# Adaptive layer norm, Koopman attention and 4-bit feed-forward in one kernel: feed-forward output as features by tokens and turned back on TensorE, the inverse in a buffer of its own, a shorter basis and a shorter rounding

## The reference

```python
sa, ca, ga, sb, cb, gb = mod[:, 0], ..., mod[:, 5]
h = _layernorm(x) * (1 + ca) + sa
x = x + ga * attention(h)
h = _layernorm(x) * (1 + cb) + sb
x = x + gb * ffn(h)
```

```python
G = Kc.T @ Kc + RIDGE_EPS * I
W = jnp.linalg.solve(G, Kc.T @ Vc)
U = U0
for _ in range(POWER_K):
    U, _ = jnp.linalg.qr(W @ U)
Wr = U @ (U.T @ W)
S_new = DECAY_ALPHA * S + Wr
out = SCALE * (Qc @ S_new)
```

```python
gate = fp4_linear(x, w_gate)
y = fp4_linear(x, w_up)
h = jax.nn.silu(gate) * y
return fp4_linear(h, w_down)
```

## Time and profile before

| | us |
|---|---|
| median of three runs | 1487.51 |
| lowest, highest | 1479.54, 1488.72 |
| the profiled execution | 1489.35 |
| its span, first to last instruction | 1487.5 |
| TensorE busy | 969.3 (65%) |
| VectorE busy | 1230.2 (83%) |
| ScalarE busy | 640.3 (43%) |
| GpSimd busy | 231.3 (16%) |

### The profile page before, as it was taken

How to read it: one execution, slowest core, us unless ns; L and a number is a source line. 1 busy time by engine, 2 the same in 40 slices (tenths; PEclk the granted TensorE clock), 3 DMA queues, 4 the chain that set the end, 5 groups by cost and what they waited for, 6 DMA issues and landing times.

```text
span 1487.5 us, 43627 instructions
## 1 busy us (share of the span) xinstructions
PE 969.3 (65%) x17726; PEld 780.0 (52%) x17726; DVE 1230.2 (83%) x3729; ACT 640.3 (43%) x1294; POOL 231.3 (16%) x149
## 2 busy tenths in 40 slices
PE   1443940389177799787799787852819825996175
PEld 0332530365167667677667686742717624775154
DVE  5885659949999779996799996798875798878997
ACT  3663630156135466555466454431416512563152
POOL 3552001101111001113102023012140000021000
PEclk9855985589579899899899898785959957898597
DMA  2555110001000001001101002030030200111000
GB/s 78 168 167 194 46 44 0 1 18 50 8 4 4 4 10 46 2 4 50 54 17 38 3 4 86 4 123 0 4 125 19 75 1 17 50 47 32 9 25 24
DMA packets 52086, 61.60 MB, mean 41 GB/s; under 512 B 4048, under 2 KB 32416, under 8 KB 51888
## 3 DMA queue, kind: packets, MB, share of 16 engines
q1 hardware_dynamic: 51888, 58.84, 12.6%
HBM read 38.31 MB, written 20.51 MB: 40 GB/s over the span
## 4 chain that ended last, share of the span: by engine, by line
DVE 36%; PE 32%; issue 13%; ACT 5%; POOL 2%; DMA 1%; SPq 0%; DVEq 0%; POOLq 0%; ACTq 0%
PE a_bank L840 5%; PE a_bank L830 3%; PE a_bank L846 3%; DVE a_total L1581 3%; DVE a_outer L1579 3%; DVE a_blocks L1584 3%; DVE a_outer L1575 2%; PE a_bank L946 2%; PE a_bank L961 2%; PE a_bank L769 2%; PE a_bank L898 2%; PE a_bank L698 2%; DVE a_blocks L1586 2%; DVE a_recip L1561 2%; PE a_bank L808 2%
## 5 line engine op out<-in xcount | busy, mean ns | idle before, releaser
L1092 ACT ACTIVATE a_work<-a_bank 128x512 f32<-128x512 f32 (+1 forms) x193 | 110.9, 599 | 206.5 <-PE a_bank L808 170.8
L1485 POOL TENSOR_TENSOR a_root<-a_recip,a_half 128x32 f32<-128x32 f32 (+2 forms) x24 | 89.8, 3743 | 655.8 <-DVEq L1570 636.9
L808 PE MATMUL a_bank<-a_ident,a_blocks 128*128 128x128 f32 x256 | 42.2, 340 | 162.6 <-DVE a_blocks L1595 162.6
L1092 ACT ACTIVATE a_solve<-a_bank 128x512 f32<-128x512 f32 (+2 forms) x184 | 87.9, 522 | 114.1 <-PE a_bank L846 53.9
L1575 DVE TENSOR_TENSOR a_outer<-a_blocks,a_weight 128x62 f32<-128x62 f32 (+15 forms) x248 | 129.4, 522 | 0.0
L1581 DVE TENSOR_REDUCE a_total<-a_outer 128x62 f32<-128x62 f32 (+30 forms) x248 | 127.0, 512 | 0.3
L808 PEld LDWEIGHTS a_bank<-a_ident,a_blocks 128*128 128x128 f32 x256 | 40.4, 208 | 163.7 <-DVE a_blocks L1595 163.7
L1579 DVE TENSOR_TENSOR a_outer<-a_blocks 128x60 f32<-128x60 f32 (+14 forms) x240 | 119.2, 497 | 0.7 <-DVE a_outer L1575 0.7
L1584 DVE TENSOR_TENSOR a_blocks<-a_blocks,a_outer 128x60 f32<-128x60 f32 (+14 forms) x240 | 118.3, 493 | 0.0
L698 PE MATMUL a_bank<-a_wk,a_cg 128*128 128x512 f32 x256 | 117.3, 602 | 0.0
L769 PE MATMUL a_bank<-a_scaled,a_blocks 128*128 128x352 f32 x256 | 90.6, 495 | 28.7 <-ACT a_scaled L1072 15.2
(11 more groups left out here) (200 smaller groups left out, 2402.4 us busy)
## 6 DMA issues: line engine op xcount, KB each, us to landing
f_x<-in_L_attn_x SPq DMA_DIRECT2D x16, 256.0 KB, 3.2
s_xnt<-f_xt SPq DMA_DIRECT2D x16, 256.0 KB, 2.1
s_c<-f_cm SPq DMA_DIRECT2D x16, 256.0 KB, 2.3
s_base<-f_base SPq DMA_DIRECT2D x16, 256.0 KB, 2.8
a_cg<-s_c SPq DMA_DIRECT2D x16, 256.0 KB, 2.9
a_cc<-s_c SPq DMA_DIRECT2D x16, 256.0 KB, 3.7
a_xnt<-s_xnt SPq DMA_DIRECT2D x16, 256.0 KB, 3.9
a_base_in<-s_base SPq DMA_DIRECT2D x13, 256.0 KB, 2.6
```

Of the source, the lines that this page charges most:

```text
L808: last = nc.tensor.transpose(bank[:, i * P:(i + 1) * P], rows_[:, :, 4 * rb + i], ident[:])
L1092: nc.scalar.activation(out, view, ACT.Copy, scale=scale).then_inc(emptied, 1)
L1485: nc.gpsimd.tensor_tensor(root[:, :, a:b], recip[:, :, a:b], half[:, :, a:b], ALU.pow).then_inc(roots_ok, 1)
```

## The change

Four things change.

1. In `factor` the inverse gets a buffer of its own, `triangle`, cleared and given ones on its diagonal before the wait for the block. The weights are gone: the known rows are multiplied with `m[:, :, 0:i, i]`, numbers that earlier steps left in the matrix, one in each column. The 31 memsets are gone, and one product scales the whole result.
2. `orthogonalise` takes the square of the vector and its products with the rest in one pass, and divides the few results, not the vector.
3. `fp4_blocks` drops one instruction: the bound and the magic number go into the addition and the subtraction.
4. Feed-forward `down` makes its output as features by tokens, 512 columns at once; ScalarE scales it by `gb`, which is now a number for each partition, and TensorE adds it, turned back, onto the residual, which it has put into the bank by a product with the identity. `finish` is gone from VectorE. The step `down` is cut in two, `turn_hidden` (t) and `down` (y), and the order becomes g0, g1, t0, g2, y0, t1, g3, y1 and so on, where it was g0, g1, d0, g2, d1.

```diff
-                        row, rest = m[:, :, 0:j, j], m[:, :, 0:j, i:HB]
                         ch.wait(inverse)
...
-                        weights = ch.inc(V.scalar_tensor_tensor(weight[:, :, 0:i], m[:, :, i, 0:i], -1.0, recip[:, :, 0:i], ALU.mult, ALU.mult))
-                        column = ch.inc(V.scalar_tensor_tensor(m[:, :, j, i:HB], m[:, :, i:HB, j], -1.0, bcast(recip[:, :, j], 2, n_i), ALU.mult, ALU.mult))
-                        ch.wait(weights)
-                        terms = area(0, n_i, i)
-                        known = ch.inc(V.tensor_tensor(terms, m[:, :, i:HB, 0:i], bcast(weight[:, :, 0:i], 2, n_i), ALU.mult))
-                        if j:
-                            ch.wait(column)
-                            step = area(2 * KEPT * KEPT, j, n_i)
-                            product = ch.inc(V.tensor_tensor(step, bcast(m[:, :, j, i:HB], 2, j), bcast(row, 3, n_i), ALU.mult))
+                        ch.link(V.scalar_tensor_tensor(m[:, :, j, i:HB], m[:, :, i:HB, j], -1.0, bcast(recip[:, :, j], 2, n_i), ALU.mult, ALU.mult))
+                        terms, step = area(0, n_i, i), area(2 * KEPT * KEPT, i, n_i)
+                        known = ch.inc(V.tensor_tensor(terms, m[:, :, i:HB, 0:i], bcast(m[:, :, 0:i, i], 2, n_i), ALU.mult))
+                        product = ch.inc(V.tensor_tensor(step, bcast(m[:, :, j, i:HB], 2, i), bcast(x[:, :, 0:i, j], 3, n_i), ALU.mult))
                         ch.wait(known)
                         summed = ch.inc(V.tensor_reduce(total[:, :, 0:n_i], terms, op=ALU.add, axis=AX_X))
-                        if j:
-                            ch.wait(product)
-                            ch.inc(V.tensor_tensor(rest, rest, step, ALU.add))
+                        ch.wait(product)
+                        ch.inc(V.tensor_tensor(x[:, :, 0:i, i:HB], x[:, :, 0:i, i:HB], step, ALU.add))
...
-                    for i in range(1, HB):
-                        V.memset(m[:, :, i, 0:i], 0.0)
-                    ch.link(V.memset(diagonal, 1.0))
                     dve.wait_ge(roots_ok, n * 3)
-                    V.tensor_tensor(m[:, :, 0:KEPT], m[:, :, 0:KEPT], bcast(root[:], 2, KEPT), ALU.mult)
-                    V.tensor_tensor(m[:, :, KEPT:HB, KEPT:HB], m[:, :, KEPT:HB, KEPT:HB], bcast(root[:, :, KEPT:HB], 2, KEPT), ALU.mult).then_inc(done, 1)
+                    V.tensor_tensor(m, x, bcast(root[:], 2, HB), ALU.mult).then_inc(done, 1)
...
-                        sq = prod[:, 0:2 * DH].rearrange("p (s d) -> p s d", s=2)
-                        ch.link(V.tensor_tensor(sq, u, u, ALU.mult))
-                        ch.link(V.tensor_reduce(norm[:], sq, op=ALU.add, axis=AX_X))
+                        ch.link(V.tensor_tensor(flat(pr), flat(left), bcast(u.rearrange("p s d -> p (s d)"), 1, n), ALU.mult))
+                        ch.link(V.tensor_reduce(dots[:, 0:n], pr, op=ALU.add, axis=AX_X))
...
-    each(lambda v, amax, scale, inv, step: V.tensor_scalar(step, step, 1.0, 1.5 * 2.0 ** 22, ALU.max, ALU.mult))
-    each(lambda v, amax, scale, inv, step: V.tensor_tensor(v, v, step, ALU.add))
+    each(lambda v, amax, scale, inv, step: V.scalar_tensor_tensor(v, step, ROUNDER, v, ALU.max, ALU.add))
...
             def down(self, b):
...
+                x = xs[b % 3] if b < EARLY else xc[:, NC * (b - EARLY):NC * (b - EARLY) + NC]
+                self.u.need(self.at["hht"])
+                bank = self.u.fill()
+                for k, (at, n) in enumerate(FI_CHUNKS):
+                    last = nc.tensor.matmul(bank[:], w_dn[0:n, k], hht_[0:n, k], start=(k == 0), stop=(k == NW - 1))
+                self.done(last)
...
+                bank = self.u.fill()
+                nc.tensor.matmul(bank[:], ident[:], x.rearrange("p t d -> p (t d)"), start=True, stop=False, skip_group_check=True)
                 self.u.need(m)
-                bank = self.u.fill()
                 for t in range(NC):
-                    for k, (at, n) in enumerate(FI_CHUNKS):
-                        last = nc.tensor.matmul(bank[:, t * P:(t + 1) * P], hht[0:n, k, t], w_dn[0:n, k], start=(k == 0), stop=(k == NW - 1))
+                    last = nc.tensor.matmul(bank[:, t * P:(t + 1) * P], yt[:, t * P:(t + 1) * P], ident[:], start=False, stop=True,
+                                            skip_group_check=True)
...
+            def down(self, b):
+                bank = self.u.empty()
+                nc.scalar.activation(yt, bank[:], ACT.Identity, scale=gb[:, b:b + 1]).then_inc(emptied, 1)
...
-            steps = [("g", 0)] + [(kind, b + (kind == "g")) for b in range(B - 1) for kind in "gd"] + [("d", B - 1)]
+            steps = [("g", 0), ("g", 1)] + [(kind, b + 2 * (kind == "g")) for b in range(B) for kind in "tgy" if kind != "g" or b + 2 < B]
```

More of the change, by code:

```diff
@@ L574, in main_pass @@
         outer_all = sb("outer", [P, 4 * KEPT * HB])
-        weight, total = sb("weight", [P, 2, HB]), sb("total", [P, 2, HB])
+        total, triangle = sb("total", [P, 2, HB]), sb("triangle", [P, 2, HB * HB])
         cg = [sb(f"cg{i}", [P, NC, D]) for i in range(2)]
@@ L749, in turn_rows @@
                 self.done(last)
+                bank = self.u.fill()
+                self.done(nc.tensor.transpose(bank[:, 0:B], gb_rows, ident[0:B, 0:B]))
                 self.at["rows"] = self.u.mark()
@@ L1306, in ffn @@
             for kind, b in steps:
-                yield from (e.gate_up if kind == "g" else e.down)(b)
+                yield from {"g": e.gate_up, "t": e.turn_hidden, "y": e.down}[kind](b)
         def units(steps):
-            return sum(GATE_UNITS if kind == "g" else DOWN_UNITS for kind, b in steps)
+            return sum({"g": GATE_UNITS, "t": NW, "y": 2}[kind] for kind, b in steps)
         def last_group(e, g):
@@ L1546, in _, with factor @@
                 dve.sem_inc(cc_used, 1)
-                def factor(block_, n, done):
-                    m = by_columns(block_)
-                    diagonal = block_[:, :, 0:HB * HB:HB + 1]
+                def factor(block_, n, given, done):
+                    m, x = by_columns(block_), by_columns(triangle[:])
+                    diagonal, ones = (y[:, :, 0:HB * HB:HB + 1] for y in (block_, triangle))
                     def area(at, a, b):
@@ L1561, in pivot @@
                         return ch.inc(V.reciprocal(recip[:, :, j], m[:, :, j, j]))
+                    ch.link(V.memset(triangle[:], 0.0))
+                    ch.inc(V.memset(ones, 1.0))
+                    dve.wait_ge(*given)
                     ch.link(V.tensor_scalar(diagonal, diagonal, RIDGE_EPS, None, ALU.add))
```

101 lines of the change are left out of this document (49 added, 52 removed).

## The result

The changed kernel takes 1529.69 us (median of four runs, 1525.8 to 1531.74), the kernel before 1488.12 in the same session: a ratio of 1.029, 95% interval 1.025 to 1.033. The profiled execution has a span of 1527.5 us. The forecast was 1548.5 with a range of 1508 to 1575, so sign and range held, and the time is 19 us too high.

What follows compares the result with a forecast made beforehand. VectorE was taken to bound the factor stages and feed-forward batches, TensorE the batches afterwards. Five factors +60.5, leads +18.0 and feed-forward -17.5 summed to +61 on 1487.51: 1548.5 us, range 1508 to 1575.

Steps and rivals of the forecast that it cites:

- The sign: Whole kernel: slower, by +61 us or 4%; chance of slower 0.86.
- Removed weight: Each step of `factor`: dropping the weight instruction earns 0, between -0.4 and +0.5 us, as the column is then waited for.
- Own buffer: In `factor`: the inverse's separate buffer lengthens outer product and addition by 2.1 us, +1.7 a factor after fewer waited starts.
- the final product: End of `factor`: one multiply of 2048 elements takes 2.29 us, +0.47, still waiting for GpSimd's last roots.
- Strided operand: Known-row products in `factor`: a second operand read 128 bytes apart costs 9.9 us more a factor, bounds 5.4 and 10.8.
- The leads: Three lead factors beside TensorE: each 14.0 us longer, 42.0 less 24.0 slack, adding 18.0 us to the path.
- The basis: `orthogonalise`: shorter rounds save 4.1 us, only the last one being on the path.
- Feed-forward: All feed-forward: -17.5 us, of which last stage -11.4, middle -4, stretch before the last basis -2.
- rival B: Feed-forward: TensorE keeps up with VectorE and batches run at 11.3 us, giving 1530 us; chance 0.08.
- A: `factor`: strided reads cost nothing in long operands, so 1481 us, no measurable change; chance 0.11.
- C: Free strided reads in `factor` together with TensorE keeping up in feed-forward: 1462 us, 1.7% faster; chance 0.03.
- D: `factor`: a long strided stream costs a third cycle an element, some 20 us a factor, giving 1630 us; chance 0.05.

Runs made afterwards that it cites:

- the base: Also called e1: the changed kernel with the whole old `factor` put back, all else as changed; 1460.36 us, ratio 0.980 to the kernel before.
- e2: The changed kernel with the known rows multiplied by side-by-side weights again, the inverse keeping its own buffer; 1473.90 us, ratio 0.990 to the kernel before.
- e5: The kernel before with only the shorter basis and shorter rounding; `factor`, `down` and `finish` as before; 1472.00 us, ratio 0.986.
- e12: The kernel before with shorter basis and rounding, old `down` cut in two in the new order, `finish` on VectorE; 1482.24 us, ratio 0.994.
- e8: The changed kernel with old `factor`, and also the old `orthogonalise` put back; 1470.27 us, ratio 0.984 to the kernel before.
- e4: The changed kernel with old `factor`, its weights stored 32 elements (128 bytes) apart in all eight factors; 1514.55 us, ratio 1.017.
- e3: The changed kernel with old `factor`, its weights stored 2, 4, 8 or 32 elements apart depending on the stage; 1489.44 us, ratio 1.001.

## Why the prediction was right, and where it was not

**The sign** was right for the reason given: the strided operand. It is 54 to 56 of the 69 us by which the new factor makes the base slower, the own buffer some 14.

**Removed weight, 0.** Right (+0.2 a factor, and e2, which puts it back, has the factor that the theory without any price for it gives). The Trainium skill's rule ("VectorE: DVE Perf Modes", Rules for kernel authors), to minimise the number of operations and not the semaphores, would have given 6 us a factor, and here the trace disagrees: the removed instruction overlapped its neighbour (3.57 us from start to start for 6.15 us of work), and that neighbour is now waited for. The same page of the Trainium skill (The DRAIN you can't avoid) says that a next instruction that is not held starts earlier, and with that the trace agrees.

**Own buffer, +1.7, and the final product, +0.5.** The two longer instructions cost 2.2, the final product is 2.29 us as worked out, the roots are waited for as before. e2's factor is 2.7 longer than the base's, against 2.2.

**Strided operand, +9.9 a factor.** The main term that was mis-sized: 7.5. The step that failed is "from 32 to 62 elements the strided form grows by 2.03 ns an element, against 1.04", carried to 512: at 512 the excess is 1054 - 687 = 367 ns, 0.72 an element. Two points 30 elements apart, each read to a few ns, were no slope for a tenfold length, and its "first 30 elements are hidden" is no property of length either: the known product of the last step, 62 elements read once each, takes 0.26 us where it took 0.22 in line, 0.6 ns an element already (see also the last section). The bounds of 5.4 and 10.8 did hold it. The five factors on the path grew by 9.6 to 10.5 us each, 50.6 in all, where 60.5 was forecast: 9.9 us of the error.

**The leads, +18.0.** The three stretches from the end of a Schur factor to the start of the next grew by 6.8, 2.1 and 3.2 us, 12.1 in all. Counted from the end of the Schur factor, the leads ended 12.2, 11.3 and 11.4 us later; less the slack of 24.0, the step's own working gives 11.0. The returns, which the prediction kept out of the sum and in the range, were 2.0, 2.2 and 0.8 us longer; with them it gives 16.0. The 12.1 can't decide between the two: in ten profiles with the factor of before (before, e1 and e5 to e12) the three stretches sum to 390.3 to 401.2 us, so that one difference of two profiles is uncertain by several us.

**The basis, -4.1.** Right: 3.97 in e8.

**Feed-forward, -17.5 in all.** -24.1 in fact: the stretch before the last basis -4.5 (-2 predicted), from there to the end of the last input preparation -4.5 (-4), behind it -15.2 (-11.4, of a window that began 15 us later). "TensorE's round 13.1" came to 12.44: the down part takes 4.5 from L807 to L795, not 5.0, because ScalarE's scaled copy is covered by the identity product. "So TensorE becomes the bound, and a batch gains 0.4 us, not the 2.2 of VectorE" is the step that failed: a distance between batches on one engine was taken for the pace of the stage. The slower engine had work in hand, so that VectorE ran at its own 11.3 through all of six batches; rival B's pace came true on VectorE while TensorE's stayed near the forecast. The margin was small: where TensorE lost 2.3 to 2.5 us at a lower clock (e8, e4), it did become the bound, from the fourth batch on. And the order, which the prediction credited with 0.8 us a batch and charged 2.8 for the fourth `gate_up`, is worth 15 with the new `down`.

**Rivals.** A and C fall with e3 (strided reads cost), D with the 1054 ns; B's sum, 1530, is what was measured, but that is chance: the factor was 2 us cheaper, and TensorE did not come at 11.3.

## What to carry to other kernels

Before saving an instruction on an in-order engine, look at its start and its neighbour's: if they overlap, it costs less than its duration, and a new wait in its place can take all of it; then ask how the remaining operands are laid out, since 10,912 products a factor with each second operand 128 bytes from the last cost 7.5 us more, where the weights had cost 3.6 to make. The period of the slower engine is the pace of a stage only after what it holds in hand is used up; over a few batches both engines' ends have to be followed to the last one. And where work leaves an engine, look at what may then be put later in the queue of another: moving `finish` off VectorE paid only together with the gate product ahead of `down`, and the gate product ahead only without `finish`.

## What the runs showed of the hardware

A long VectorE product costs 1.34 ns an element in line at 512 (687 ns, fixed part included) and 2.0 to 2.15 (1032 to 1097 ns) with the second operand 16 bytes or more apart; 8 bytes apart costs nothing (16.22 against 16.21 us). Beyond 16 bytes distance lowers the price slightly, if at all: in one and the same factor 4 elements cost 0.50 us more than 32, and 8 cost 0.76 more. The price also differs with the factor, 23.4 to 24.4 us for the eight of e4 at distance 32, where the products in line take 16.2 in all eight; why is not shown. Writing up to 62 elements 16 bytes or more apart makes an instruction of 0.20 us 0.02 longer. And whether the price is paid at all depends on how many far elements the inner row has. The known product in the kernel after, first Schur factor, with rows of 3, 4, 28 and 29 far elements:

```profile
341.29 0.34 DVE L1611 TENSOR_TENSOR a_outer<-a_blocks 128x174 f32<-128x174 f32 x1
343.06 0.54 DVE L1611 TENSOR_TENSOR a_outer<-a_blocks 128x224 f32<-128x224 f32 x1
...
415.26 0.54 DVE L1611 TENSOR_TENSOR a_outer<-a_blocks 128x224 f32<-128x224 f32 x1
417.21 0.45 DVE L1611 TENSOR_TENSOR a_outer<-a_blocks 128x174 f32<-128x174 f32 x1
```

The same 174 elements take 0.34 us when a row of three is read 29 times (0.33 in line) and 0.45 when a row of 29 is read three times (0.34 in line); with rows of four the full price is there, 0.54 against 0.39 in line. What holds the three is not shown by these runs.
